# Grouping the residual adds of the last stage behind the eighth sub-block of each token tile

## The chip, the cores and the metric

The kernel runs on all 8 cores of one Trainium2 chip. Each core takes 1,024 of the 8,192 tokens; the cores exchange nothing. The metric is the device time in microseconds of the slowest core; before the change it is 1675.8 us (median of two runs, 1673.51 and 1678.10).

## The reference, cut to what matters

```python
xn = _layernorm(x, axis=-1)
x = x + attn(xn, Wq, bq, Wk, bk, Wv, bv) + ffn(xn, weight, bias, lora_A, lora_B, lora_start_indices)
# attn: q, k, v = xn @ Wq, Wk, Wv + bias ; 32 query heads, 8 key/value heads
scores = einsum('bsdh,bseh->bsde', q, k) / sqrt(128)     # per token: 128 x 128
out    = einsum('bsde,bseh->bsdh', softmax(scores, -1), v)   # per token: 128 x 32
```

The attention is within a token: for each token a 128 x 128 matrix of scores between the feature positions, its softmax, and a product with the values. The feed-forward part is one 4096 x 4096 linear layer with a small adapter. Both are added to x.

## The kernel before, in words

The program of a core is one function, `build`, that writes a stream of instructions for each engine, with semaphores by hand (VEC counts VectorE's instructions, TEN TensorE's groups, SCA ScalarE's, and so on). Phases 1 to 4 normalise x, transpose it, and make q, k and v and the feed-forward output. q and k go to a scratch tensor in HBM, v stays on chip in `vall`, and the feed-forward output stays on chip in `ffno` as fp16. The change touches only phase 5.

Phase 5 goes over 8 tiles (`tt`) of 128 tokens. A tile has 4 chunks (`ck`) of 32 tokens, and a chunk two sub-blocks of 16 tokens, so a tile has eight sub-blocks (`sub` 0 to 7; `vs` counts them over all tiles). The engines work as follows.

- TensorE, for each chunk: 8 groups of score products into two PSUM buffers `s_ps` (L778), then 32 pairs of products, values into `a_ps` (L795) and row sums into `b_ps` (L798), two buffers each, one per sub-block. The products of sub-block `vs` wait until VectorE has multiplied sub-block `vs - 2` (`vmark_mult`, L791).
- ScalarE turns each group of scores into `ebf` with an exponential (L817).
- VectorE, for each sub-block: a reciprocal (L829) and a multiplication of `a_ps` into one eighth of `tmpa_full` (L834; 512 of its 4,096 columns). After sub 3 and after sub 7 it adds one half of the tile, 128 x 2048: `tmpa_full` into `xasm` (L847), then `ffno` into `xasm` (L853). `xasm` holds the tile's x, three buffers in turn (the first is `xasm_e`). The add after sub 3 first waits until both halves of x have been loaded (semaphore XS, L845).
- The queue of SyncE (SP) issues the loads of q and k of each chunk (L723, L725), two chunks ahead: for chunk `cki` it waits for the scores of chunk `cki - 2` (L721). After the loads of a tile's last chunk it issues the store of half 0 of the tile two back (`emit_out`, L710 to L716, waits for `vmark_half0`, signals OD). The last two tiles' stores follow the loop.
- The queue of GpSimd (POOL) issues, for each tile, the two loads of x (L753), then the store of half 1 of the tile two back (`emit_out1`, L735 to L742, waits for `vmark_tile`, signals OG). From tile 3 on the loads first wait for both stores of the tile three back (L750, L751), whose buffer they reuse. The last two tiles' stores follow the loop.

Each load or store of half a tile moves 1 MB in runs of 32 floats, since x is laid out by token and `xasm` by feature position. In what follows out0 and out1 are the stores of half 0 and half 1, and out1(5) is that of tile 5.

Of the kernel before, what the change touches and what calls it, by code (L numbers as in the profile page):

```python
# [13 lines left out]
ALU = mybir.AluOpType  # L14
# [19 lines left out]
def build(taps=DEBUG_TAPS, phases=5):  # L34
# [26 lines left out]
    with ExitStack() as ctx:  # L61
# [39 lines left out]
        XS = [S(ctx, nc, f"XS{i}") for i in range(3)]  # L101
# [3 lines left out]
        VEC = S(ctx, nc, "VEC")  # L105
# [12 lines left out]
        @block.gpsimd  # L118
        def _(g):
            g.dma_start(out=id_sb[:], in_=id_d).then_inc(GQ.h, 16)  # L120
            g.dma_start(out=bq_sb[:], in_=bq_d).then_inc(GQ.h, 16)
            g.dma_start(out=bk_sb[:], in_=bk_d).then_inc(GQ.h, 16)
            g.dma_start(out=bv_sb[:], in_=bv_d).then_inc(GQ.h, 16)
            g.dma_start(out=fb_sb[:], in_=fb_d).then_inc(GQ.h, 16)
            g.dma_start(out=lsi_sb[:], in_=lsi_d).then_inc(GQ.h, 16)
            g.dma_start(out=bsel_sb[:], in_=bsel_d).then_inc(GQ.h, 16)
            GQ.n += 7 * 16
            for ft in range(2):
                g.dma_start(out=wsl[ft][:].rearrange("p (c f) -> p c f", f=P),
                            in_=wall[ft].rearrange("(c p) f -> p c f", p=P))\  # L130
                    .then_inc(WQ[ft].h, 16)
                WQ[ft].n += 16
# [442 lines left out]
        ffno = ctx.enter_context(nc.sbuf_tensor("ffno", [P, TPC * 32], FP16, side="right"))  # L575
# [86 lines left out]
        vmark_half0 = {}  # L662
        vmark_tile = {}
        nv = p5_vec0
        for tt in range(NT):
            for sub in range(8):
                nv += 2
                vmark_mult[tt * 8 + sub] = nv
                if sub == 3:
                    nv += 2  # L670
                    vmark_half0[tt] = nv
            nv += 2
            vmark_tile[tt] = nv
        p5_vec_end = nv
# [4 lines left out]
        def xs_mark(tt):  # L679
            return 32 * (tt // 3 + 1)  # L680
# [4 lines left out]
        with ExitStack() as p5ctx:  # L685
            def p5sb(n_, s_):
# [4 lines left out]
            xasm = [xasm_e] + [  # L691
                p5ctx.enter_context(nc.sbuf_tensor(f"xasm{i}", [P, P * 32], F32, side="right"))
                for i in range(1, 3)]
            tmpa_full = p5ctx.enter_context(
                nc.sbuf_tensor("tmpa_full", [P, 4096], F32, side="right"))
# [126 lines left out]
            @block.vector  # L822
            def _(v):
                v.wait_ge(SCA.h, p4_sca_end)
                for tt in range(NT):
                    for sub in range(8):
                        vs = tt * 8 + sub
                        v.wait_ge(TEN.h, ten_osub(vs // 2, vs % 2))
                        v.reciprocal(rdb[:, (sub % 2) * 16:(sub % 2) * 16 + 16],  # L829
                                     b_ps[vs % 2][:]).then_inc(VEC.h, 1)  # L830
                        v.wait_ge(VEC.h, VEC.n + 1)
                        rdv = rdb[:, (sub % 2) * 16:(sub % 2) * 16 + 16]\
                            .unsqueeze(2).broadcast_to([P, 16, 32])
                        v.tensor_tensor(  # L834
                            tmpa_full[:, sub * 512:(sub + 1) * 512]
                            .rearrange("p (t h) -> p t h", h=32),
                            a_ps[vs % 2][:].rearrange("p (t h) -> p t h", h=32),
                            rdv, ALU.mult).then_inc(VEC.h, 1)
                        VEC.n += 2
                        assert VEC.n == vmark_mult[vs]  # L840
                        if sub == 3 or sub == 7:
                            hf = sub // 4
                            lo, hi = hf * 2048, (hf + 1) * 2048
                            if sub == 3:
                                v.wait_ge(XS[tt % 3].h, xs_mark(tt))  # L845
                            v.wait_ge(VEC.h, VEC.n)
                            v.tensor_tensor(xasm[tt % 3][:, lo:hi],  # L847
                                            xasm[tt % 3][:, lo:hi],
                                            tmpa_full[:, lo:hi], ALU.add)\
                                .then_inc(VEC.h, 1)  # L850
                            VEC.n += 1
                            v.wait_ge(VEC.h, VEC.n)
                            v.tensor_tensor(xasm[tt % 3][:, lo:hi],  # L853
                                            xasm[tt % 3][:, lo:hi],
                                            ffno[:, tt * 4096 + lo: tt * 4096 + hi],
                                            ALU.add).then_inc(VEC.h, 1)
                            VEC.n += 1
                            assert VEC.n == (vmark_half0[tt] if sub == 3
                                             else vmark_tile[tt])

            @block.sync
            def _(sy):
# [64 lines left out]
```

## Time and profile before

| what | value |
|---|---|
| median of the runs (two) | 1675.8 us |
| the profiled execution, its own time | 1677.76 us |
| its span on the slowest core (core 6) | 1676.1 us |
| spans of the 8 cores | 1654.6 to 1676.1 us |
| TensorE busy | 1389.7 us, 83% |
| VectorE busy | 261.2 us, 16% |
| ScalarE busy | 498.4 us, 30% |
| phase 5 on core 6 | about 1334 to 1676 us |

The table's busy times are of the whole span. Phase 5 is the last fifth of it, and its engines look different from the rest: in the page's row of slices TensorE falls from nine tenths busy to between five and eight, with its clock in half. Since the change is in phase 5 alone, its views are read from 1335 us on.

### The profile page before, as it was taken

The page shows a single profiled execution, that of the slowest core. Times are in us where ns is not written, and L with a number is a line of the kernel's source. Part 1 is how long each engine was busy: PE and PEld are TensorE (multiplying, and loading weights), DVE is VectorE, ACT ScalarE, POOL GpSimd, SP SyncE. Part 2 cuts the span into 40 slices and gives each one's busy share as a digit, 9 for nine tenths or more (in the row PEclk, how much of TensorE's full clock was granted, in tenths as well). Part 3 has the DMA queues.
Part 4 walks back from the last instruction along what each step waited for, and adds up shares of the span by engine and source line. Part 5 has one row for each costly group of instructions (what it writes and reads, how often), then busy time and mean ns, then how long its engine had stood idle before and what let it go on. Part 6 is the DMA issues. An engine that isn't in the chain of part 4 may idle for free.

```text
span 1676.1 us, 20262 instructions; the slowest of 8 cores (1654.6 to 1676.1 us)
## 1 busy us (share of the span) xinstructions
PE 1389.7 (83%) x8705; PEld 691.1 (41%) x8705; DVE 261.2 (16%) x260; ACT 498.4 (30%) x496; POOL 265.0 (16%) x135
## 2 busy tenths in 40 slices
PE   1227899999999999999879999999999778655550
PEld 0113344444444444444334444444444356534440
DVE  6893200000000000000000000000000045422342
ACT  2553001100111033333333333333333356444440
POOL 6441011111111111111001111111101210111121
PEclk9999999999999999999969999999999955555555
DMA  9411977777777777777647777677777776878898
GB/s 229 152 72 11 85 76 75 76 75 76 76 77 77 78 78 77 79 76 79 71 90 75 76 73 70 68 72 70 76 75 76 87 98 85 115 96 109 113 122 113
DMA packets 440470, 144.76 MB, mean 86 GB/s; under 512 B 433136, under 2 KB 433168, under 8 KB 439312
## 3 DMA queue, kind: packets, MB, share of 16 engines
q0 software_dynamic: 340032, 109.92, 62.0%
q1 hardware_dynamic: 100352, 33.56, 11.4%
q8 instruction: 71, 1.16, 0.3%
q14 instruction: 15, 0.12, 0.0%
HBM read 207.20 MB, written 20.97 MB: 136 GB/s over the span
## 4 chain that ended last, share of the span: by engine, by line
PE 70%; issue 12%; DMA 8%; DVE 4%; ACT 2%; POOL 2%; POOLq 0%; SPq 0%; ACTq 0%; DVEq 0%
PE qk_ps L426 39%; PE f_ps L610 27%; DMA out<-xasm 2%; PE s_ps L778 2%; DMA out<-xasm_e 1%; DVE lnst L227 1%; DMA qkscr<-tsb 1%; DMA wsl<-wall 1%; DVE lnst L216 1%; PE f_ps L615 1%; POOL xasm L753 1%; ACT ebf L817 1%; DVE lnst L212 1%; DMA kst<-qkscr 1%; PE xa_ps L441 1%
## 5 line engine op out<-in xcount | busy, mean ns | idle before, releaser
L426 PE MATMUL qk_ps<-xnT,wsl 128*128 128x512 bf16 x3072 | 667.3, 380 | 6.5 <-DMA wsl<-wall 5.5
L426 PEld LDWEIGHTS qk_ps<-xnT,wsl 128*128 128x128 bf16 x3072 | 301.3, 98 | 371.8 <-issue 12.3
L610 PE MATMUL f_ps<-xnT,wsl 128*128 128x512 bf16 x2048 | 449.9, 380 | 1.9 <-ACT tsb L550 1.9
L610 PEld LDWEIGHTS f_ps<-xnT,wsl 128*128 128x128 bf16 x2048 | 198.3, 98 | 251.2 <-issue 18.4
L642 ACT ACTIVATE ffno<-f_ps,fb_sb 128x512 f16<-128x512 f32 x64 | 152.5, 2629 | 299.0 <-PE f_ps L615 299.0
L829 DVE RECIPROCAL rdb<-b_ps 128x16 f32<-128x16 f32 x64 | 16.1, 252 | 1220.6 <-PE b_ps L798 1220.5
L778 PE MATMUL s_ps<-qst,kst 8*128 8x128 bf16 x1024 | 136.2, 299 | 67.3 <-ACT ebf L817 38.2
L817 ACT ACTIVATE ebf<-s_ps 128x512 bf16<-128x512 f32 x256 | 140.0, 594 | 149.0 <-PE s_ps L778 148.4
L379 POOL DMA_DIRECT2D wsl<-wall x46 | 77.2, 1679 | 590.5 <-PE qk_ps L426 577.8
L465 ACT ACTIVATE qsks<-qk_ps,bqss 128x512 bf16<-128x512 f32 x16 | 36.8, 2535 | 373.7 <-PE qk_ps L426 373.7
L778 PEld LDWEIGHTS s_ps<-qst,kst 8*128 8x128 bf16 x1024 | 90.8, 126 | 105.5 <-issue 92.7
L593 POOL DMA_DIRECT2D wsl<-wall x32 | 53.6, 1676 | 457.4 <-PE f_ps L615 433.1
L283 PE MATMUL tr_ps<-id_sb,xn 128*128 128x128 bf16 x256 | 33.8, 302 | 109.0 <-ACT xn L258 99.8
L795 PE MATMUL a_ps<-vall,ebf 128*128 128x32 bf16 x1024 | 60.3, 188 | 52.0 <-DVE tmpa_full L834 51.3
L795 PEld LDWEIGHTS a_ps<-vall,ebf 128*128 128x128 bf16 x1024 | 56.7, 104 | 57.8 <-issue 57.8
L283 PEld LDWEIGHTS tr_ps<-id_sb,xn 128*128 128x128 bf16 x256 | 22.9, 130 | 119.6 <-issue 116.3
L199 POOL TENSOR_TENSOR sqscr<-xt 128x2048 f32<-128x2048 f32 x16 | 57.3, 3600 | 54.1 <-DVE lnst L212 51.1
L481 ACT ACTIVATE vall<-qk_ps,bv_sb 128x512 bf16<-128x512 f32 x16 | 38.3, 2642 | 72.4 <-PE qk_ps L426 72.4
L798 PE MATMUL b_ps<-vall,ebf 128*128 128x1 bf16 x1024 | 59.1, 165 | 0.0
L481 ACT ACTIVATE qsks<-qk_ps,bk_sb 128x512 bf16<-128x512 f32 x16 | 36.7, 2528 | 73.8 <-PE qk_ps L426 73.8
L798 PEld LDWEIGHTS b_ps<-vall,ebf 128*128 128x128 bf16 x1024 | 57.0, 104 | 0.7 <-issue 0.7
L753 POOL DMA_DIRECT2D xasm<-x_in x10 | 27.5, 2752 | 117.2 <-issue 68.5
(70 smaller groups left out, 464.5 us busy)
## 6 DMA issues: line engine op xcount, KB each, us to landing
wsl<-wall POOLq DMA_DIRECT2D x80, 1024.0 KB, 10.0
xt<-x_in SPq DMA_DIRECT2D x8, 2048.0 KB, 8.9
xasm<-x_in POOLq DMA_DIRECT2D x10, 1024.0 KB, 14.4
xasm_e<-x_in POOLq DMA_DIRECT2D x6, 1024.0 KB, 14.8
out<-xasm SPq DMA_DIRECT2D x5, 1024.0 KB, 13.9
out<-xasm POOLq DMA_DIRECT2D x5, 1024.0 KB, 12.4
qkscr<-tsb SPq DMA_DIRECT2D x16, 256.0 KB, 2.6
out<-xasm_e POOLq DMA_DIRECT2D x3, 1024.0 KB, 12.4
```

Of the source, the lines that this page charges most:

```text
L199: g.tensor_tensor(sq2[h][:], xt[tt % 3][:, h * 2048:(h + 1) * 2048], xt[tt % 3][:, h * 2048:(h + 1) * 2048], ALU.mult).then_inc(PL.h, 1)
L283: tr = t.transpose(tr_ps[b4 % 2][:, c * P:(c + 1) * P], xnt_[tt % 2][:, cc * P:(cc + 1) * P], id_sb[:])
L379: g.dma_start(out=wsl[ft % 2][:].rearrange("p (c f) -> p c f", f=P), in_=wall[ft].rearrange("(c p) f -> p c f", p=P))\
L426: mm = t.matmul(qk_ps[bank + half][:], wsl[ft % 2][:, c * P:(c + 1) * P], xnT[:, c * TPC + half * 512: c * TPC + (half + 1) * 512], start= ...
L481: s.activation(dst, qk_ps[bank + half][:], AF.Identity, bias=bias).then_inc(SCA.h, 1)
L593: g.dma_start(out=wsl[ft % 2][:].rearrange("p (c f) -> p c f", f=P), in_=wall[ft].rearrange("(c p) f -> p c f", p=P))\
L610: t.matmul(f_ps[bank + half][:], wsl[ft % 2][:, c * P:(c + 1) * P], xnT[:, c * TPC + half * 512: c * TPC + (half + 1) * 512], start=(c == ...
L642: s.activation(fv[:, half * 512:(half + 1) * 512, hh], f_ps[bank + half][:], AF.Identity, bias=fb_sb[:, hh:hh + 1]).then_inc(SCA.h, 1)
L778: mm = t.matmul(s_ps[gidx % 2][:, k4 * P:(k4 + 1) * P], kst[cki % 2][:, ts * P:(ts + 1) * P], qst[cki % 2][:, ts * P:(ts + 1) * P], start= ...
L795: t.matmul(a_ps[vs % 2][:, (ts % 16) * 32:(ts % 16) * 32 + 32], ebf[cki % 2][:, ts * P:(ts + 1) * P], vrep, start=True, stop=True)
L798: mmb = t.matmul(b_ps[vs % 2][:, ts % 16:ts % 16 + 1], ebf[cki % 2][:, ts * P:(ts + 1) * P], vall[:, tok * 9 + 8:tok * 9 + 9], start=True, ...
L817: s.activation(ebf[cki % 2][:, g * 512:(g + 1) * 512], s_ps[gidx % 2][:], AF.Exp).then_inc(SCA.h, 1)
```

## The change

VectorE's adds of the first half of a tile move from behind sub 3 to behind sub 7. All eight reciprocals and multiplications of a tile now come first, and the four adds follow in a row: half 0 (`tmpa_full`, then `ffno`), half 1 (the same). The wait for the loads of x moves with the first add. The marks `vmark_half0` and `vmark_tile`, for which the two stores wait, are counted anew. No instruction is added or dropped, and the other engines' streams are the same but for the values of the marks.

```diff
             for sub in range(8):
                 nv += 2
                 vmark_mult[tt * 8 + sub] = nv
-                if sub == 3:
-                    nv += 2
-                    vmark_half0[tt] = nv
+            nv += 2
+            vmark_half0[tt] = nv
             nv += 2
             vmark_tile[tt] = nv
...
                         assert VEC.n == vmark_mult[vs]
-                        if sub == 3 or sub == 7:
-                            hf = sub // 4
-                            lo, hi = hf * 2048, (hf + 1) * 2048
-                            if sub == 3:
-                                v.wait_ge(XS[tt % 3].h, xs_mark(tt))
-                            v.wait_ge(VEC.h, VEC.n)
-                            v.tensor_tensor(xasm[tt % 3][:, lo:hi],
-                                            xasm[tt % 3][:, lo:hi],
-                                            tmpa_full[:, lo:hi], ALU.add)\
-                                .then_inc(VEC.h, 1)
-                            VEC.n += 1
-                            v.wait_ge(VEC.h, VEC.n)
-                            v.tensor_tensor(xasm[tt % 3][:, lo:hi],
-                                            xasm[tt % 3][:, lo:hi],
-                                            ffno[:, tt * 4096 + lo: tt * 4096 + hi],
-                                            ALU.add).then_inc(VEC.h, 1)
-                            VEC.n += 1
-                            assert VEC.n == (vmark_half0[tt] if sub == 3
-                                             else vmark_tile[tt])
+                    for hf in range(2):
+                        lo, hi = hf * 2048, (hf + 1) * 2048
+                        if hf == 0:
+                            v.wait_ge(XS[tt % 3].h, xs_mark(tt))
+                        v.wait_ge(VEC.h, VEC.n)
+                        v.tensor_tensor(xasm[tt % 3][:, lo:hi],
+                                        xasm[tt % 3][:, lo:hi],
+                                        tmpa_full[:, lo:hi], ALU.add)\
+                            .then_inc(VEC.h, 1)
+                        VEC.n += 1
+                        v.wait_ge(VEC.h, VEC.n)
+                        v.tensor_tensor(xasm[tt % 3][:, lo:hi],
+                                        xasm[tt % 3][:, lo:hi],
+                                        ffno[:, tt * 4096 + lo: tt * 4096 + hi],
+                                        ALU.add).then_inc(VEC.h, 1)
+                        VEC.n += 1
+                        assert VEC.n == (vmark_half0[tt] if hf == 0
+                                         else vmark_tile[tt])
```

## Rows read from the trace of the kernel before

**Rows 1.** Waits of phase 5: engine line waited for, total us, times, longest.

```profile
DVE xasm L847 <- DMA xasm<-x_in: 58.9, 3, 22.4
PE a_ps L795 <- DVE tmpa_full L834: 51.3, 4, 16.5
DVE xasm_e L847 <- DMA xasm_e<-x_in: 24.4, 2, 20.5
```

**Rows 2.** Timeline of GpSimd's queue: start us, us, instruction, [idle before, releaser].

```profile
1424.30 2.76 POOL L753 DMA_DIRECT2D xasm_e<-x_in  x1 [31.52 <-DMA out<-xasm_e]
...
1453.22 2.77 POOL L737 DMA_DIRECT2D out<-xasm  x1 [10.89 <-issue]
1470.34 2.75 POOL L753 DMA_DIRECT2D xasm<-x_in  x1 [14.35 <-DMA out<-xasm]
1485.54 2.76 POOL L753 DMA_DIRECT2D xasm<-x_in  x1 [12.45 <-issue]
1503.70 2.76 POOL L737 DMA_DIRECT2D out<-xasm  x1 [15.41 <-issue]
1516.79 2.76 POOL L753 DMA_DIRECT2D xasm<-x_in  x1 [10.33 <-DMA out<-xasm]
1531.75 2.75 POOL L753 DMA_DIRECT2D xasm<-x_in  x1 [12.20 <-issue]
...
1620.78 2.75 POOL L753 DMA_DIRECT2D xasm<-x_in  x1 [11.63 <-issue]
1633.51 2.77 POOL L737 DMA_DIRECT2D out<-xasm  x1 [9.99 <-issue]
1650.61 2.76 POOL L737 DMA_DIRECT2D out<-xasm_e  x1 [14.33 <-issue]
1663.32 2.76 POOL L737 DMA_DIRECT2D out<-xasm  x1 [9.95 <-issue]
```

**Rows 3.** Timeline of SyncE's queue: the stores of half 0 of tiles 0, 1, 2, 6, 7.

```profile
1413.44 0.41 SPq L712 DMA_DIRECT2D out<-xasm_e  x1
...
1446.94 0.40 SPq L712 DMA_DIRECT2D out<-xasm  x1
...
1481.71 0.40 SPq L712 DMA_DIRECT2D out<-xasm  x1
...
1614.79 9.88 SPq L712 DMA_DIRECT2D out<-xasm_e  x1
1638.13 0.37 SPq L712 DMA_DIRECT2D out<-xasm  x1
```

**Rows 4.** Timeline of VectorE: adds of tiles 1, 4 and 7.

```profile
1401.50 2.29 DVE L847 TENSOR_TENSOR xasm<-xasm,tmpa_full 128x2048 f32<-128x2048 f32 x1
...
1503.56 2.29 DVE L847 TENSOR_TENSOR xasm<-xasm,tmpa_full 128x2048 f32<-128x2048 f32 x1 [19.62 <-DMA xasm<-x_in]
1505.95 2.29 DVE L853 TENSOR_TENSOR xasm<-xasm,ffno 128x2048 f32<-128x2048 f32 x1
1508.16 0.25 DVE L829 RECIPROCAL rdb<-b_ps 128x16 f32<-128x16 f32 x1
1508.52 0.69 DVE L834 TENSOR_TENSOR tmpa_full<-a_ps,rdb 128x512 f32<-128x512 f32 x1
...
1633.37 2.29 DVE L847 TENSOR_TENSOR xasm<-xasm,tmpa_full 128x2048 f32<-128x2048 f32 x1 [16.84 <-DMA xasm<-x_in]
...
1644.86 2.29 DVE L853 TENSOR_TENSOR xasm<-xasm,ffno 128x2048 f32<-128x2048 f32 x1
```

**Rows 5.** Chain of waits: where TensorE begins the value products of two successive chunks.

```profile
1398.33 0.14 PE a_ps L795
...
1405.46 0.14 PE a_ps L795
```

**Rows 6.** Stages: us; busy PE, PEld, DVE, ACT, POOL; PEclk, DMA share, GB/s.

```profile
1485.00:1503.00 18.00, 10.48 (x128) 7.44 (x128) 0.00 (x0) 9.01 (x16) 2.76 (x1) 0.50 0.94 122
...
1663.00:1676.00 13.00, 0.00 (x0) 0.00 (x0) 0.00 (x0) 0.00 (x0) 2.76 (x1) 0.50 0.58 81
```

## The prediction

> **What bounds the kernel now.** The change lies in phase 5, so I read that stage, beginning with the waits. They show the thing the change touches: VectorE stood before its first add of a tile for 58.9 + 24.4 = 83.3 us in five stops, until the load of x had landed, and behind it TensorE stood for 51.3 us in four stops because `a_ps` was not free [rows 1]. A stop on the busiest engine looks like the price of the stage. Whether it is depends on what sets the loads, so the next view is the timeline of GpSimd's queue, and the reader is to see there that it never rests from 1424.30 us to the end [rows 2].
>
> In that queue a load or store of half a tile holds up the next one for about 13 us or more. A cycle of tile 4 runs: loads at 1470.34 and 1485.54, out1(2) at 1503.70, and the loads of tile 5 at 1516.79. The last of these waited for the landing of out1(2), issued only just before, because they reuse its buffer. So the cycle has three transfers in single file: 15.2 + 18.2 + 13.1 = 46.5 us [rows 2]. TensorE needs 1405.46 - 1398.33 = 7.13 us for a chunk, 28.5 us for a tile, when nothing stops it [rows 5]. The queue is the slower of the two by 18 us in each tile, and the waits of [rows 1] are what is left over on the faster side. The tail says the same: loads of tile 7 until 1633.51, then out1(5), out1(6), out1(7) at 1633.51, 1650.61 and 1663.32, and the span ends at 1676.1 [rows 2]. VectorE's last add began at 1644.86 and ended at 1647.15, 16.2 us ahead of the out1(7) that needed it [rows 2, 4].
>
> Phase 5 from 1424.30 us on is thus ten loads and seven out1 stores in a row on one queue, 251.8 us. Its start is set by out0(0), which SyncE issued at 1413.44 and whose landing released GpSimd after an idle time of 31.5 us [rows 2, 3].
>
> **The change part by part.** *The adds themselves.* 32 adds of 2.29 us before and after, nothing added. What moves is two adds per tile, from the middle to the end.
>
> *The wait for x, moved.* VectorE no longer stops after sub 3. TensorE can finish the tile and go into the next one: it stops when it wants the third sub-block of the next tile, whose buffer needs sub 0 multiplied. So it runs two chunks further ahead than now, up to 14.3 us [rows 5]. The five stops of VectorE don't vanish, they move behind sub 7. Do GpSimd's loads come earlier for it? They wait for out0 and out1 of the tile three back. out1 is in GpSimd's own file, and was the later of the two: for tile 5, out0(2) was issued at 1481.71 and out1(2) at 1503.70, 22 us later [rows 2, 3]. An earlier out0 therefore releases nothing. Gain on the path: 0 us.
>
> *The marks of the stores.* In the file, out1(tt - 2) waits for `vmark_tile[tt - 2]`, a tile that VectorE finished one whole tile ago; being some 5 us later is hidden by that. Only the last tile is close. After the change all eight multiplications of tile 7 are done before its x has landed: VectorE and TensorE wait for x at 1633.37 either way. Four adds in a row take three spacings of 2.39 us (1505.95 - 1503.56) and the last 2.29, 9.5 us, so `vmark_tile[7]` comes at 1642.8 instead of 1647.15 [rows 4]. out1(7) is at 1663.32 and has 20.5 us to spare instead of 16.2: 0 us. `vmark_half0[7]` follows two adds after x in both kernels, so out0(7) stays at 1638.13: 0 us.
>
> *The burst at a tile's end.* In tiles 0 to 2 x is there in time, so the four adds run right behind sub 7 and can stop TensorE. This is the one place upstream of the file: out0(0) is issued behind the scores of the second chunk of tile 2. From tile 1's end: first add at 1401.50 [rows 4], next reciprocal 3 x 2.39 + 2.21 = 9.38 us later, multiplication 0.36 us after it and 0.69 us long, sub 0 of tile 2 free at 1411.93. TensorE wants that buffer with its next chunk's value products, at 1405.46 + 7.13 = 1412.59 [rows 5]. The cover is 0.66 us: thin, but it holds in each of the tiles, since the pace is the same. Cost: 0 us. Were the cover gone altogether, each of the two boundaries ahead of out0(0) would cost at most the two added adds, 4.8 us, together 9.6 us. The pace that gives the cover is of a granted clock of 0.50 [rows 6], the lower of the two levels, 1.2 GHz. TensorE is no busier on average after the change, so I take it to stay there.
>
> *What the DMA engines share.* Half-tile transfers slow each other. Alone, out1(7) left the DMA share at 0.58, while load and stores of tile 4 together had 0.94 [rows 6]. A step of the file was 13.1 us for out1(2) without an out0 beside it. It was 17.1 for out1(1) and 17.1 for out1(5), each with an out0 in flight (1446.94, 1614.79 and 1638.13) [rows 2, 3]. Loads took 12.7 (1620.78 to 1633.51) to 18.2 us. SyncE issues an out0 behind the scores of a tile's second chunk. As TensorE runs two chunks further ahead, out0(3) to out0(6) go some 14 us or more earlier (an estimate from the 7.13 us pace: out0(6) near 1600 instead of 1614.79), and they meet other steps: the last three would run beside out1(3) and out1(4) more than now, which I take to have 13.1 us steps as out1(2) has. Upper bound: three such stores lose 4.0 us each and nothing comes back, +12 us. Lower bound: three loads go from 15.0 (1516.79 to 1531.75) to 12.7 and a fourth from 15.2, with no loss elsewhere, 3 x 2.3 + 2.5 = -9.4 us. The bytes are the same and the file is never idle, so what one step loses another gets back; I take 0 us, between the two.
>
> The Trainium skill, page "DMA: Bandwidth & Descriptors", section "Queues, rings and completion order", says that each DMA engine takes turns between the queues that have work for it, packet by packet. By that rule an out0 costs the file its share wherever it lies, which gives the same 0 us. The trace agrees in part: the 13.1 and 17.1 us steps differ with company, but the 12.7 us step had company too.
>
> *Sum.* 0 + 0 + 0 + 0 + 0 on a span of 1676.1 us, and its own time 1677.76 with the 1.7 us around it. That execution was 2.0 us above the median of the runs, 1675.8, so the median to expect is 1676 us.
>
> **The rivals.**
>
> *The stop was the price.* If TensorE's 51.3 us lay on the path, taking them away would end at 1677.8 - 51.3 = 1626 us. For it: the waits [rows 1], and that the load's wait is moved off the middle. Against it: a queue that is never idle behind its own stores.
>
> *The burst shows.* If VectorE is 0.7 us later than worked out at the two early boundaries, TensorE waits, out0(0) goes later, and the whole file starts later: up to +9.6 us, 1685 us. It decides from a chunk pace under 6.5 us. This is the mechanism that ends on the slow side. For it: a cover of only 0.66 us. Against it: all spacings come from one steady pattern.
>
> *Stores collide.* The upper bound of the sharing, +12 us, 1688 us. For it: out1(1) and out1(5). Against it: the loads are relieved at the same time.
>
> *Loads are relieved.* The lower bound, -9 us, 1667 us.
>
> *The burst starves the queue.* The first add of a tile starts as x lands, just when GpSimd issues an out1. If adds hold up that engine's issue, then the 4.8 us by which the burst grows is added in each of tiles 3 to 7, 5 x 4.8 = +24 us, 1700 us. Against it: out1(2) was issued at 1503.70 in the middle of an add (1503.56 to 1505.85) and took 2.76 us, as the others did, and its step of 13.1 us is among the shortest [rows 2, 4]. The Trainium skill, page "SBUF — State Buffer", section "SBUF: two separate sides", says that a VectorE operation in a two-port mode locks GpSimd out of a shared port pair, so that it can't write DMA descriptors. By that rule the issue would have been held up here, if these adds ran in such a mode; the row shows that they did not hold it up.
>
> **How the numbers follow.** Forecast, nothing beyond a few us of shuffling (1669 to 1683 us): 0.72. Stores collide: 0.10. Loads relieved: 0.08. The burst shows: 0.05. The stop was the price: 0.03. The queue starved: 0.02, half of it at more than 2%, if the loads' issues are held up as well. The predicted time is that of the first, 1676 us. The range takes in the bounds that carry weight, -9 and +10 us: 1666 to 1686 us; outside lie the first and last rival and most of the colliding stores. A measurement of this kernel can tell about 2% from no change, 33.5 us, so only the first rival is faster (0.03) and half of the last slower (0.01); I give 0.02 to slower for what I haven't seen, and 0.95 to the same.
>
> **What would show each step.** In the changed kernel's trace: GpSimd's queue without rest from about 1424 to the end, and out1 last. VectorE's stops before its first add smaller by the head start of two chunks at least, 50 to 70 us in all, and each behind a multiplication of sub 7. TensorE's stops on `a_ps` not gone but smaller, and at the third sub-block of a tile. out0(0) still about 11 us ahead of GpSimd's 31.5 us release, and no TensorE stop on VectorE before it. Steps of out1(3) and out1(4) at 15 to 17 us, loads of tile 7 at 13. Four adds spaced 2.39 us. I am wrong if the file's total departs from 252 us by more than 10, if a cycle shrinks with its transfers unchanged, or if TensorE waits for VectorE before 1413 us.

## The result, and the profile after

The changed kernel took 1689.0 us (median of 17 runs) against 1676.5 us for the kernel before (16 runs). Over undisturbed runs the ratio is 1.0064, 95% interval 1.0047 to 1.0082: slower by some 11 us. It is within the 2% of "the same", but outside the predicted range of 1666 to 1686 us, and a clear loss where none was forecast. (The medians include runs in which one die ran slower; ratios do not.)

The profiled execution after took 1692.2 us, its slowest core is core 3 with a span of 1690.6 us, the others have 1667.6 to 1678.7. One core against another mixes in chance (before the change the file took 239.0 to 251.8 us, core by core), so the following table has means over all eight cores of the one profiled execution, worked out from the timelines of GpSimd, SyncE and VectorE of each core. "File" is GpSimd's row of loads and stores from the first load of tile 3 to the end of the span, a step is the time from one issue in it to the next, and a cycle is the two loads of a tile and the out1 behind them; "load 6a" is the first load of x of tile 6.

| step, mean of 8 cores, us | before | after |
|---|---|---|
| from VectorE's first reciprocal to out0(0) | 67.6 | 68.4 |
| cycle 3: loads 3a, 3b, out1(1) | 15.1, 13.6, 17.0 | 14.1, 13.3, 17.1 |
| cycle 4: loads 4a, 4b, out1(2) | 13.9, 15.1, **13.1** | 13.9, 14.7, **15.6** |
| cycle 5: loads 5a, 5b, out1(3) | 13.9, 15.7, **13.2** | 15.3, 15.5, **15.8** |
| cycle 6: loads 6a, 6b, out1(4) | 13.8, 15.4, **13.1** | 16.6, 14.0, **18.9** |
| cycle 7: loads 7a, 7b, out1(5) | 14.3, 12.8, 17.3 | 14.6, 11.8, 16.1 |
| out1(6), out1(7) to the end | 25.4 | 25.4 |
| the whole file | 242.8 | 252.8 |

The file, which was predicted to keep its length, grew by 10.0 us, and the stretch ahead of it by 0.8. That is the measured loss. The file grew in out1(2) to out1(4) by 2.5, 2.6 and 5.8 us and in the first loads of tiles 5 and 6 by 1.4 and 2.8. Cycle 3 was 1.1 us shorter, and the last cycle gave only 1.8 us back.

GpSimd's timeline on core 3 after the change (start us, length, instruction, idle time before and its releaser) answers to [rows 2]:

```profile
1589.89 2.76 POOL L752 DMA_DIRECT2D xasm_e<-x_in  x1 [13.38 <-issue]
1603.75 2.76 POOL L736 DMA_DIRECT2D out<-xasm  x1 [11.11 <-issue]
1623.66 2.76 POOL L752 DMA_DIRECT2D xasm<-x_in  x1 [17.15 <-DMA out<-xasm]
1637.63 2.75 POOL L752 DMA_DIRECT2D xasm<-x_in  x1 [11.22 <-issue]
1649.37 2.77 POOL L736 DMA_DIRECT2D out<-xasm  x1 [8.99 <-issue]
```

Out1(4), issued at 1603.75, held the file for 19.9 us. The next two rows, the loads of tile 7, took 14.0 and 11.7 us. SyncE's stores on the same core, answering to [rows 3], say who kept it company:

```profile
1555.02 0.42 SPq L711 DMA_DIRECT2D out<-xasm  x1
...
1603.77 0.42 SPq L711 DMA_DIRECT2D out<-xasm  x1
1608.37 8.69 SPq L711 DMA_DIRECT2D out<-xasm_e  x1
1653.98 0.37 SPq L711 DMA_DIRECT2D out<-xasm  x1
```

Out0(5) went out at 1603.77, in the same moment as out1(4), and out0(6) 4.6 us later, behind the second add of tile 6. Before, both lay beside the loads of tile 7, where they started 8 us into the first of them, issued at 1606.39 [rows 2]. SyncE's rows of that time, from core 6 of the kernel before:

```profile
1614.30 0.40 SPq L712 DMA_DIRECT2D out<-xasm  x1
1614.79 9.88 SPq L712 DMA_DIRECT2D out<-xasm_e  x1
```

Out0(6) started 4.6 us into out1(4) on all eight cores of the changed kernel. The x of tile 6 lands as GpSimd issues out1(4), VectorE's adds of tile 6 follow, and out0(6) waits for the first two of them. Out0(5) started from 0.0 to 2.5 us into out1(4) on seven cores.

VectorE's adds of tile 5 on core 3, the burst (answering to [rows 4]):

```profile
1557.78 2.29 DVE L845 TENSOR_TENSOR xasm<-xasm,tmpa_full 128x2048 f32<-128x2048 f32 x1 [16.97 <-DMA xasm<-x_in]
1560.17 2.29 DVE L851 TENSOR_TENSOR xasm<-xasm,ffno 128x2048 f32<-128x2048 f32 x1
1562.57 2.29 DVE L845 TENSOR_TENSOR xasm<-xasm,tmpa_full 128x2048 f32<-128x2048 f32 x1
1565.32 2.29 DVE L851 TENSOR_TENSOR xasm<-xasm,ffno 128x2048 f32<-128x2048 f32 x1 [0.46 <-DVE xasm L845]
1567.53 0.25 DVE L828 RECIPROCAL rdb<-b_ps 128x16 f32<-128x16 f32 x1
```

And the waits of phase 5 (engine, line, waited for: total us, times, longest), answering to [rows 1]:

```profile
DVE xasm L845 <- DMA xasm<-x_in: 34.5, 2, 17.5
...
PE a_ps L794 <- DVE tmpa_full L833: 26.1, 2, 14.7
...
DVE xasm_e L845 <- DMA xasm_e<-x_in: 17.4, 1, 17.4
```

VectorE's waits for x fell from 83.3 to 51.9 us and TensorE's for VectorE from 51.3 to 26.1 us, while the kernel became slower. Both engines stood less, and the time did not follow. On the other cores both waits shrank as well.

The windows of the last full cycle, tile 7's two loads and out1(5), show that the DMA engines were less busy there. First the kernel before (core 6), then after (core 3); columns as in [rows 6], the last three being the granted clock, the DMA share and GB/s:

```profile
1606.00:1650.00 44.00, 20.29 (x356) 16.08 (x353) 17.32 (x21) 14.16 (x26) 8.27 (x3) 0.50 1.10 142
```

```profile
1624.00:1665.00 41.00, 5.19 (x91) 3.93 (x88) 11.53 (x9) 4.32 (x8) 7.93 (x3) 0.50 0.69 105
```

Before, the share was 1.10 there; after, 0.69, since two of the three out0 stores and all loads of q and k had already gone by. The granted clock was 0.50 in both. The work was pulled into earlier cycles. Their steps got longer by more than this one got shorter.

### The profile page after: what moved, and what is told of

The parts are those of the page before. It is cut to its first block, busy times and chain, and to the rows that moved or that the text cites. A ratio compares the mean times of both kernels' runs of the same rounds, so it can differ in the third digit from the quotient of the medians.

```text
span 1690.6 us, 20262 instructions; the slowest of 8 cores (1667.6 to 1690.6 us)
## 1 busy us (share of the span) xinstructions
PE 1390.3 (82%) x8705; PEld 690.7 (41%) x8705; DVE 261.1 (15%) x260; ACT 498.1 (29%) x496; POOL 264.9 (16%) x135
## 4 chain that ended last, share of the span: by engine, by line
PE 69%; issue 12%; DMA 9%; DVE 4%; ACT 2%; POOL 2%; POOLq 0%; SPq 0%; DVEq 0%; ACTq 0%
PE qk_ps L426 39%; PE f_ps L610 27%; DMA out<-xasm 3%; DMA kst<-qkscr 2%; DMA out<-xasm_e 1%; PE s_ps L777 1%; DVE lnst L227 1%; DMA qkscr<-tsb 1%; DMA wsl<-wall 1%; DVE lnst L216 1%; PE f_ps L615 1%; POOL xasm L752 1%; DVE lnst L212 1%; ACT ebf L816 1%; PE xa_ps L441 1%
## 5 line engine op out<-in xcount | busy, mean ns | idle before, releaser
L610 PEld LDWEIGHTS f_ps<-xnT,wsl 128*128 128x128 bf16 x2048 | 198.5, 98 | 251.5 <-issue 18.9
L794 PE MATMUL a_ps<-vall,ebf 128*128 128x32 bf16 x1024 | 60.4, 188 | 27.2 <-DVE tmpa_full L833 26.1
## 6 DMA issues: line engine op xcount, KB each, us to landing
xasm<-x_in POOLq DMA_DIRECT2D x10, 1024.0 KB, 14.6
out<-xasm SPq DMA_DIRECT2D x5, 1024.0 KB, 15.5
out<-xasm_e POOLq DMA_DIRECT2D x3, 1024.0 KB, 14.7
```

The costliest lines, as they stand in the source:

```text
L610: t.matmul(f_ps[bank + half][:], wsl[ft % 2][:, c * P:(c + 1) * P], xnT[:, c * TPC + half * 512: c * TPC + (half + 1) * 512], start=(c == ...
L794: t.matmul(a_ps[vs % 2][:, (ts % 16) * 32:(ts % 16) * 32 + 32], ebf[cki % 2][:, ts * P:(ts + 1) * P], vrep, start=True, stop=True)
```

## The experiments

Two theories stood at the start. Theory A: the head start of TensorE and SyncE puts SyncE's stores of half 0 beside GpSimd's stores of half 1, which collide. Theory B: the burst of four adds slows the out1 beside it. "File" is again the mean over eight cores, of one profiled execution of each kernel. The cores of a kernel differ by a standard deviation of 1.4 to 4.3 us, which makes 0.5 to 1.5 us for a mean of eight, so differences of 1 to 2 us between two files say little. Ratios are of many runs, against the kernel before on the same chip.

| kernel | file, us | cycles 4, 5, 6, 7 | ratio, 95% |
|---|---|---|---|
| before | 242.8 | 42.2, 42.8, 42.3, 44.3 | 1 |
| changed | 252.8 | 44.2, 46.6, 49.5, 42.5 | 1.0064 (1.0047 to 1.0082) |
| e1: x waited for behind sub 3 | 248.0 | 43.0, 45.8, 44.6, 43.5 | 1.0037 (1.0014 to 1.0059) |
| e2: burst split | 253.6 | 43.8, 48.7, 48.4, 42.1 | 1.0058 (1.0041 to 1.0076) |
| e3: stores later, tile 2 on | 254.3 | 50.4, 44.4, 43.8, 44.3 | 1.0059 (1.0041 to 1.0078) |
| e4: before, out0 beside out1 | 262.8 | 47.2, 45.8, 47.9, 46.4 | 1.0092 (1.0067 to 1.0118) |
| e5: before, out0 small | 235.1 | 41.1, 41.8, 40.0, 40.6 | 0.9936 (0.9913 to 0.9959) |
| e6: changed, out0 small | 236.3 | 43.7, 42.4, 42.1, 36.9 | 0.9949 (0.9925 to 0.9972) |
| e9: out0 held to the load | 251.9 | 44.6, 46.1, 45.8, 44.6 | 1.0059 (1.0033 to 1.0086) |
| e12: stores later, tile 3 on | 248.2 | 43.4, 46.4, 43.5, 44.2 | 1.0043 (1.0027 to 1.0058) |
| e13: e1, stores one chunk later | 243.7 | 44.5, 44.3, 42.8, 41.3 | 0.9995 (0.9979 to 1.0010) |

### e1: the wait for x back behind sub 3

```diff
                         assert VEC.n == vmark_mult[vs]
+                        if sub == 3:
+                            v.wait_ge(XS[tt % 3].h, xs_mark(tt))
                     for hf in range(2):
                         lo, hi = hf * 2048, (hf + 1) * 2048
-                        if hf == 0:
-                            v.wait_ge(XS[tt % 3].h, xs_mark(tt))
```

> The changed kernel, but VectorE again waits for x behind sub 3; the four adds stay together behind sub 7. So TensorE and SyncE lose their head start, and the burst of four adds stays. Theory A (head start: SyncE's stores of half 0 come earlier and run beside GpSimd's stores of half 1): the mean steps of out1(2), out1(3), out1(4) go back from 15.6, 15.8 and 18.9 us to about 13 us, the file from the loads of tile 3 to the end of the span from 252.8 back to about 243 us, the time to 1676 to 1680 us (out0(7) comes some 8 us later than before, which may cost a little at the end). Theory B (the longer burst of adds holds up the out1 that is issued beside it): in this kernel the burst of a tile ends behind sub 7, so what remains of it keeps the steps of out1 above 15 us, and the time at 1687 us.

By the file about half of the loss went: 248.0 us. The ratio, 1.0037, points the same way, but its interval overlaps that of the changed kernel. Out1(4) fell from 18.9 to 15.4 us, but out1(3) only to 15.2, and the first load of tile 6 stayed at 16.6. Neither theory had that. The head start is about half of it; something that remains in this kernel is the other half.

### e2: the burst cut in two

```diff
                         assert VEC.n == vmark_mult[vs]
+                        if sub == 1 and tt >= 1:
+                            adds(tt - 1, 1)      # half 1 of the tile before
...
+                    adds(tt, 0)
+                adds(NT - 1, 1)
```

> The changed kernel with its head start kept, but the burst cut in two: half 1's two adds follow sub 1 of the next tile. Theory A: out1 steps stay at 15.5 to 19 us, file near 253 us, time 1685 to 1690 us. Theory B: only two adds run as an out1 is issued, as before the change, so the steps fall to 13 us and the time to 1676 us.

The file stayed at 253.6 us. Out1(4) on the slowest core, with half the burst:

```profile
1595.72 2.76 POOL L739 DMA_DIRECT2D out<-xasm  x1 [10.66 <-issue]
1615.57 2.76 POOL L755 DMA_DIRECT2D xasm<-x_in  x1 [17.10 <-DMA out<-xasm]
```

Out0(5) had been issued at 1596.35, 0.6 us behind it. The step took 19.9 us, as with the whole burst. Theory B falls.

### e3: the stores of half 0 two chunks later

```diff
-                    if cki % 4 == 3 and cki // 4 >= 2:
+                    if cki in (11, 15):
                         emit_out(cki // 4 - 2)
+                    if cki % 4 == 1 and cki // 4 >= 5:
+                        emit_out(cki // 4 - 3)
+                sy.wait_ge(TEN.h, ten_schunk(4 * NT - 1))
+                emit_out(NT - 3)
                 emit_out(NT - 2)
                 emit_out(NT - 1)
```

> The changed kernel, VectorE untouched, but SyncE issues the stores of half 0 of tiles 2 to 5 two chunks later in its queue, which takes the head start away from the stores alone and leaves it to the loads of q and k. Theory A: they lie beside loads of x again instead of beside out1(3) and out1(4); those steps go to about 13 to 14 us; time 1676 to 1682 us. If it is the earlier loads of q and k that slow the file, or the burst (theory B), nothing changes: 1687 us.

No gain in the time, against theory A at first sight. The cycles tell more. Those of tiles 5 and 6 fell from 46.6 and 49.5 to 44.4 and 43.8 us. But my edit put out0(2), at 1508.37 on core 5, on top of out1(2):

```profile
1505.77 2.76 POOL L740 DMA_DIRECT2D out<-xasm  x1 [11.74 <-issue]
1526.71 2.76 POOL L756 DMA_DIRECT2D xasm<-x_in  x1 [18.18 <-DMA out<-xasm]
```

That step took 20.9 us, and cycle 4 went from 44.2 to 50.4. The long step moved with the store. Nor does it need the same moment: out0(2) started 2.1 to 6.0 us into out1(2), core by core, and the step took 20.9 to 21.5 us on all of them.

### e4: the collision by hand, in the kernel before

```diff
                     if cki % 4 == 3 and cki // 4 >= 2:
+                        if cki // 4 >= 4:
+                            sy.wait_ge(XS[(cki // 4) % 3].h, xs_mark(cki // 4))
                         emit_out(cki // 4 - 2)
```

> The kernel before, VectorE untouched, but from tile 4 on SyncE waits for x of tile tt before it issues out0(tt - 2), so that it starts in the same moment as out1(tt - 2): the collision by hand, without head start and without burst. Theory A: steps of out1(2) to out1(4) grow from 13.1 to 16 to 19 us, loads beside get cheaper by 1 to 2 us, the time rises by 4 to 15 us, to 1680 to 1691 us. Theory B: out1 steps stay at 13.1 us and the time at 1676 us.

Without head start or burst the file grew by 20 us, twice as much as in the changed kernel. Out1(3) on core 7, with out0(3) issued at 1548.13:

```profile
1548.31 2.77 POOL L739 DMA_DIRECT2D out<-xasm_e  x1 [11.07 <-issue]
1567.57 2.75 POOL L755 DMA_DIRECT2D xasm_e<-x_in  x1 [16.49 <-DMA out<-xasm_e]
```

It took 19.3 us instead of 13.1; the means of out1(2) to out1(4) were 20.6, 19.6 and 20.9 (expected 16 to 19), and the second loads of tiles 4 to 6 gave 2.0 to 3.3 us each back, the other loads next to nothing. Of the 20.0 us, 4.5 lie behind the last cycle, where out1(6) took 17.1 us instead of 12.7. The time, 1693.4 us, is above what I had expected (1680 to 1691).

### e5 and e6: both kernels with small stores of half 0

```diff
+                    nt_ = 64 if tt < 2 else 1
                     sy.dma_start(
-                        out=out_d[tt * P: tt * P + 64, :]
+                        out=out_d[tt * P: tt * P + nt_, :]
                         .rearrange("t (d h) -> d t h", h=32),
-                        in_=xasm[tt % 3][:, 0:2048]
+                        in_=xasm[tt % 3][:, 0:32 * nt_]
```

> The kernel before with the stores of half 0 of tiles 2 to 7 cut to one token of 64, so that part of the output is left out; the other transfers are the same. Measures what SyncE's stores cost the file. Theory A: out1(5), which had 17.3 us beside out0(6) and out0(7), falls to about 13 us; loads fall by 0 to 2 us each; time about 1660 to 1668 us.

> The changed kernel with the same stores cut (part of the output is left out). Theory A (collision of the stores): all out1 steps from out1(2) on at 13 us, and the time equal to that of the kernel before with the same cut, within 3 us. Theory B, or a cost of the earlier loads of q and k: about 10 us above it.

Both kernels leave out most of half 0 of tiles 2 to 7. This is the pair that settles what the loss needs. 1668.2 and 1668.7 us: without SyncE's stores the two kernels are equal within the intervals, file 235.1 and 236.3. The loss of 10.0 us shrinks to 1.2. So the same six stores (tiles 2 to 7) cost the file 242.8 - 235.1 = 7.7 us where the kernel before puts them, 16.5 us where the changed kernel does and 27.7 us in e4. The 1.2 us that stay are within what the cores differ by. The loads of q and k, which come earlier too, are a candidate that is not shown: counting a pair of them as beside a step when it is issued from 2 us before the step to 3 us before its end, the steps of out1(2) to out1(4) took 13.1 us with none, 13.6 with one and 14.8 with two pairs in these two kernels (48 steps), and a load of x of tiles 4 to 7 took 12.0, 13.7 and 14.3 us (128 steps). But the loads with none are all of tile 7, so that place and company can't be told apart there.

### e9: the stores held until the load of x starts

```diff
                     if cki % 4 == 3 and cki // 4 >= 2:
+                        if cki // 4 >= 4:
+                            sy.wait_ge(OG[(cki // 4) % 3].h, od_mark(cki // 4 - 3))
                         emit_out(cki // 4 - 2)
```

> The changed kernel, VectorE and head start untouched. From tile 4 on SyncE issues out0(tt - 2) only when out1(tt - 3) has landed, that is with the first load of x of tile tt, so that out0(4) and out0(5) no longer start beside an out1. Theory A (stores collide with stores; beside loads they cost less): the steps of out1(3) and out1(4) go from 15.8 and 18.9 to 14 us, loads of tiles 6 and 7 grow by 1 to 2 us, the file goes from 252.8 to about 245 to 248 us, the time from 1688 to 1679 to 1683 us. What is left above the kernel before is the loads of q and k beside out1(2) to out1(4), 1 to 2 us each. If where an out0 lies doesn't matter, the file stays at 253 us.

A miss that corrected the theory. Out1(4) went back to 13.1 us as expected and out1(3) to 14.4, but the file only to 251.9. On core 2, with out0(4) issued at 1569.82:

```profile
1570.36 2.75 POOL L754 DMA_DIRECT2D xasm_e<-x_in  x1 [11.17 <-DMA out<-xasm_e]
1589.21 2.76 POOL L754 DMA_DIRECT2D xasm_e<-x_in  x1 [16.10 <-issue]
```

The load that started together with the store took 18.9 us. The mean of load 6a was 18.6 here and 13.8 before, where out0(4) started about 8 us into it. So it is not that stores collide with stores alone: a store of half 0 that starts together with a load lengthens that load too. The cores of this kernel and of e2 show it side by side. Where out0(3) started between 0.4 us before load 5a and 1.3 us into it (five cores in each kernel), the load took 20.9 us in e2 and 19.0 in e9; where it started 3 to 5 us in (three cores in each), 13.9 and 13.6 us. The next steps return a part of that: load 5a, load 5b and out1(3) together differ by 5.7 us in e2, but only by 1.1 us in e9.

### e12: stores two chunks later, but only from tile 3 on

The edit is that of e3 with `cki in (11, 15, 19)` and `cki // 4 >= 6`.

> The changed kernel, VectorE and head start untouched; SyncE issues out0(2) where the changed kernel has it and out0(3) to out0(6) two chunks later, as the run with late stores did, which had cycles of 44.4 and 43.8 us for tiles 5 and 6 and lost its gain by putting out0(2) on out1(2). Theory A: cycles of tiles 4 to 7 at 44, 44 to 45, 44 and 44 us, out1(4) at 13 us, the file at about 247 us against 252.8, the time at 1679 to 1683 us. If only the head start of the loads of q and k, or chance, made the changed kernel slow, the file stays at 252 us or more and the time at 1687 us.

File 248.2 us: about half recovered, out1(4) at 13.1 us. Cycle 5 stayed at 46.4 us, where 44 to 45 were expected. By the ratio, 1.0043, it is a third, and its interval overlaps that of the changed kernel. On that chip the kernel before had 1680.3 us, so the 1687.4 us of this one are to be read by the ratio.

### e13: e1 with the stores where they were

In e1 the multiplications behind sub 3 are no longer pushed back by two adds. So TensorE still comes earlier to the place where SyncE may store: out0(4) started 0.9 to 1.8 us into load 6a, core by core, and 7.4 to 8.0 us into it before the change. This kernel is e1 with the stores of tiles 3 to 6 one chunk later.

```diff
+                    if cki in (11, 15, 19):
+                        emit_out(cki // 4 - 2)
+                    if cki % 4 == 0 and cki // 4 >= 6:
+                        emit_out(cki // 4 - 3)
+                sy.wait_ge(TEN.h, ten_schunk(4 * NT - 2))
```

> The kernel of the first experiment (VectorE waits for x behind sub 3, four adds behind sub 7) and, in addition, out0(3) to out0(6) one chunk later in SyncE's queue. There out0 started 1 to 5 us into the first load of x, in the kernel before 8 us into it; one chunk of 7 us puts it back where it was. Theory A2 (what costs is only where in GpSimd's file an out0 starts): the loads of tiles 6 and 7 go from 16.6 and 16.0 back to about 14 us, the file from 248.0 to 243 to 245 us, the time to within 0.2% of the kernel before. If the grouped adds cost something by themselves (theory B) or the earlier loads of q and k do, the file stays at 247 to 248 us and the time 0.3 to 0.4% above the kernel before.

Ratio 0.9995 (0.9979 to 1.0010), file 243.7: the loss is gone with all adds still grouped behind sub 7. From e1 this kernel differs only in the place of four stores, and the intervals of the two ratios do not meet. Load 6a in e1 on core 7, then in e13 on core 2:

```profile
1565.35 2.75 POOL L752 DMA_DIRECT2D xasm_e<-x_in  x1 [12.73 <-DMA out<-xasm_e]
1583.25 2.76 POOL L752 DMA_DIRECT2D xasm_e<-x_in  x1 [15.15 <-issue]
```

```profile
1568.26 2.75 POOL L756 DMA_DIRECT2D xasm_e<-x_in  x1 [12.51 <-DMA out<-xasm_e]
1581.14 2.76 POOL L756 DMA_DIRECT2D xasm_e<-x_in  x1 [10.12 <-issue]
```

17.9 us with out0(4) issued 1.0 us behind the load (1566.35), 12.9 us with it 8.2 us behind (1576.43). These two rows overstate the gain: load 6b, the next one, went from 12.6 to 14.3 us in the means, so that the two loads of tile 6 together fell from 29.1 to 27.4 us. The pairs of tiles 5 and 7 fell by 1.7 and 2.4. Not all is as before: out1(3) and out1(4) still had 15.3 and 15.4 us, and the loads of x made up for it.

### e7, e8, e10, e11: other queues

e7 (changed) and e8 (before) let SyncE issue both stores of a tile, one tile earlier; GpSimd keeps only the loads.

```diff
-                    if cki % 4 == 3 and cki // 4 >= 2:
-                        emit_out(cki // 4 - 2)
-                emit_out(NT - 2)
+                    if cki % 4 == 3 and cki // 4 >= 1:
+                        emit_out(cki // 4 - 1)
+                        emit_out1(cki // 4 - 1)
                 emit_out(NT - 1)
+                emit_out1(NT - 1)
```

> The changed kernel with both stores of a tile issued by SyncE, one tile earlier than now, so that GpSimd's file has only the loads of x. If the file of three transfers is what bounds phase 5, a cycle of 46 us goes to the larger of two loads (27 to 30 us) and TensorE's four chunks (28.5 us), some 15 us less in each of tiles 3 to 7 and the 31 us stop before tile 3 gone: 1590 to 1630 us. If SyncE's queue is held up by its own big stores, loads of q and k come late: 1640 us or more.

> The kernel before with the same two edits to the queues. With the file gone, VectorE's wait for x behind sub 3 may or may not be the next limit: if it is, this stays 5 to 20 us above the changed kernel with the same edits; if x is there in time, the two are equal within 5 us.

Ratios 0.9946 (0.9923 to 0.9969) and 0.9916 (0.9886 to 0.9946): 1669.5 and 1663.4 us. e8 is the fastest kernel of this study, 13 to 14 us under the kernel before. But both are far from the 1590 to 1630 us that "the file is the bound" had promised for e7; its second case, 1640 us or more, came in. The changed kernel comes out some 5 us above the kernel before in this setting too, though the intervals overlap. SyncE's stores of tile 5 in e8:

```profile
1586.81 0.40 SPq L712 DMA_DIRECT2D out<-xasm  x1
1587.30 13.87 SPq L721 DMA_DIRECT2D out<-xasm  x1
```

The second of two stores held the queue for 13.9 us, and GpSimd then waited for the stores to land:

```profile
POOL xasm L763 <- DMA out<-xasm: 73.3, 3, 26.4
...
POOL xasm_e L763 <- DMA out<-xasm_e: 52.8, 2, 28.6
```

So it seems bound by how fast stores and loads together get through; no run tests that. Its cycles are still some 40 us (loads of tiles 5 and 6 at 1492.44 and 1532.14), with TensorE's four chunks at 28.5.

e10 (before) and e11 (changed) only let SyncE store half 0 one tile earlier: the same diff without its two lines on `emit_out1`, and GpSimd keeps its stores.

> The kernel before, but SyncE issues the store of half 0 of the tile one back instead of two back, in the same places of its queue. out0(0) comes 28 us earlier, so the idle time of 31 us in GpSimd's queue before the loads of tile 3 shrinks to about 10 us and the file starts some 21 us earlier; later stores lie where the next tile's lay before. If the file bounds phase 5: 1652 to 1660 us. If the DMA engines' share of 0.8 to 0.9 is the real bound and the idle time is only made up elsewhere: 1665 us or more.

> The changed kernel with the same edit of SyncE's queue. The file starts some 21 us earlier too. But here out0(tt - 1) has to wait for the first two adds of tile tt - 1, which follow the landing of its x, so it is issued 5 us after out1(tt - 3) and runs beside it in every tile. Theory A: steps of out1(2) to out1(4) at 18 to 20 us, as in the collision by hand, and the time 12 to 20 us above the kernel before with the same edit. If collisions aren't the cause, the two differ by no more than the 11 us of the change itself.

Ratios 0.9954 (0.9932 to 0.9977) and 0.9951 (0.9931 to 0.9971). The file of e10 started 19.0 us earlier, counted from VectorE's first reciprocal, and was 13.0 us longer (255.8): most of the idle time that was removed came back as longer steps, as its second expectation said. e11 (file 257.1) was not slower than e10, against my expectation of 12 to 20 us. In e10 the stores also land on bad places, out1(3) had 16.7 us and load 5a 17.9, which may be why the change had nothing left to spoil; that is not shown.

## Why the prediction was wrong

- **What bounds the kernel**: right in that TensorE's and VectorE's stops were not the price. They shrank by 25 and 31 us and the kernel got slower. The file ran without rest and ended last, as told. It was only half the truth: in e7, e8 and e10, where the file is relieved, the transfers take longer and most of the gain goes.
- **The wait for x, moved**: the head start came as worked out. "Gain on the path: 0 us" held, since out0 wasn't what the loads waited for.
- **The marks of the stores**: held for tile 7. Out0(7) followed two adds behind x, and out1(7) waited for nothing (its step and that of out1(6) are 25.4 us in both).
- **The burst at a tile's end**: nothing shows that the cover of 0.66 us failed. The way to out0(0) took 68.4 against 67.6 us; no wait of TensorE for VectorE lies ahead of out0(0) on core 3, whose own 72.3 us come with 17.2 us of waits for loads of q and k, where the kernel before had 2.2 to 14.2 us, core by core.
- **What the DMA engines share**: the step that failed. Its words were "what one step loses another gets back; I take 0 us". It measured +10.0 us. The upper bound in the same paragraph, +12 us, and the rival "Stores collide" at 1688 us with a chance of 0.10 named the place and nearly the size. What was wrong is the belief that company costs the same wherever it lies. The rows read before it had a hint of the contrary: the loads of tile 7 took 14.4 and 12.7 us with two stores beside them, while out1(1) and out1(5) with company had 17.1 [rows 2, 3]. E5 puts a number on it: without those stores the two loads take 26.3 us on average instead of 27.1. The prediction saw this ("the 12.7 us step had company too") and left the sum alone. Moving those two stores away gave back 0.7 us on the two loads (27.1 to 26.4, means) and 1.2 us on out1(5), and out1(4) grew by 5.8 us. The place was also nearly certain: out0(6) can't go before two adds of tile 6, and the x that they wait for lands as out1(4) is issued, so with TensorE ahead it starts 4.6 us into that step. The prediction put it "near 1600" by TensorE's pace alone; it went at 1608.37.
- **The rule of turns between queues**: the Trainium skill, page "DMA: Bandwidth & Descriptors", section "Queues, rings and completion order", says that each DMA engine takes turns between the queues that have work for it, packet by packet; the prediction read it as "an out0 costs the file its share wherever it lies". The runs do not bear that reading out: six stores cost 7.7, 16.5 or 27.7 us by place. Whether the turns themselves are fair, no run here shows.
- **The queue starved**: refuted, by e13 and by the issues themselves. GpSimd's issues stayed at 2.75 to 2.77 us, also amid four adds.
- **The stop was the price**: refuted by the waits above.
- **The range**: "stores collide" was given too little, and the range left most of its price outside on purpose. The sign of being wrong, a file more than 10 us off 252, was set too wide for a loss of 11 us: on the slowest core the file took 259.6 us.

Of the cause this is shown: the loss needs the stores of half 0 (e5, e6), it follows their place (e3, e4, and e13 against e1), and neither the grouping nor the length of the burst makes it (e2, e13).

This stays open. No run that kept the head start and all transfers on their queues, and only moved the stores (e3, e9, e12), got back to the time of the kernel before; the best, e12, stayed at 1.0043. Whether that is places that e12 still leaves bad (out0(6) starts within 1.0 us of load 7b on all cores) or something else, such as the earlier loads of q and k together with the stores, no run separates. Why place matters is not shown either. Over the whole file a store of half 0 cost 1.3 us on average before the change, 2.8 after it and 4.6 in e4, which is less than the longest single steps suggest, since later steps give a part back. And a start some 8 us into a load is not free by itself: out0(1) started 6.7 to 9.1 us into load 3b before and after the change, core by core, and the out1(1) behind that load took 17.0 and 17.1 us. That free capacity at the seams between two transfers takes up the late store would fit with the share of 1.10 in the last cycle before, but it is only argued.

## What to carry to other kernels

When an engine off the critical path gets a head start, list every DMA that its progress triggers and look at what each will run beside; a sum of zero for "the same bytes" isn't safe, and a row where company was nearly free tells that moving it away gives little. A price that one step shows (17.1 against 13.1 us) should be charged to each step that newly gets the same company, and only what other steps show they lose with it may be taken off. A change that makes the waits of compute engines shrink says nothing of the time until the queue that ends last is measured step by step.

## What the runs showed of the hardware that I had not expected

- One 1 MB store of 128-byte runs lengthened another queue's store of the same kind by 6 to 8 us when they started together (means of 19.6 to 20.9 us in e4 against 13.1 to 13.2), and by as much when it started 2 to 6 us into it (20.9 to 21.5 us in e3).
- Beside a load the place told more: 20.9 us when the store started within 1.3 us of the load, 13.9 us when it started 4 to 5 us into it, on different cores of one execution (load 5a in e2). A part of the difference comes back in the steps behind it.
- The second of two such stores in a row held SyncE's queue for 8.7 us in the changed kernel (core 3), 9.9 us in the kernel before (core 6) and 13.9 us in e8; the first took 0.4 us.
- Steps with loads of q and k beside them, 64 KB each, were 0.5 to 2.3 us longer (13.1 to 14.8 us for an out1, 12.0 to 14.3 for a load, by none or two pairs). Since company and place went together, this is an upper reading of their price.
